# Mode weights arranged during the attention, and a depthwise buffer, its outputs and its stores laid out anew

## The chip, the cores and the metric

One core of a Trainium2 chip runs the whole program in one launch. The metric is the device time of that launch in microseconds. The engines are PE (TensorE, with its weight loads PEld), DVE (VectorE), ACT (ScalarE), POOL (GpSimd) and SP (SyncE, which here only issues transfers). All data is fp32.

## What is computed

An image `x` of 256 x 256 tokens with 128 channels passes four layers, each with a group normalization ahead of it and a residual behind it:

```python
x = x + _L0_conv_ref(_gn(x), ...)   # attention of each image row over a row of kv_x, 4 heads of 32
x = x + _L1_conv_ref(_gn(x), ...)   # 16 Fourier modes along rows and along columns, mixed by w1, w2; then an MLP
x = x + _L2_conv_ref(_gn(x), ...)   # one-channel convolutions and a pointwise chain
x = x + _L3_conv_ref(_gn(x), ...)   # two depthwise 7x7 convolutions, gate, softplus, then a product with W_out
```

Two parts matter here. In layer 1 each of 16 modes per axis multiplies by a complex 128 x 128 matrix, taken from `w1` and `w2`, whose shape is (128 in, 128 out, 16 modes, 2 parts). In layer 3 the result per token is

```python
h_final = jnp.exp(log_h[-1])        # a softplus of (conv_B(x) * sigmoid(conv_gate(x)))
return h_final @ W_out + b_out
```

## The kernel before

The stages follow one another, with a barrier of all engines between them: statistics (to about 99 us), `attention` (to 1955 us), `spectra` (to 2081 us), the mixing of modes, the MLP in two halves, the one-channel part, the pointwise part (to about 3850 us) and `depthwise_layer` (to the end).

**Attention.** One image row after the other, in a software pipeline written out by hand; PE's order, and the waits that other engines signal, set the pace. POOL does three things per row, in this order: `add_mask(n + 2, 0)`, `spread_sums(n - 1)`, `add_mask(n + 2, 1)`. SP loads `x`, `kv_x` and the mask four rows ahead and stores the row before last.

**Spectra.** SP streams the whole of `x1` (64 tiles of 512 KB, 12 in flight) while PE takes its modes along the other axis and transposes it for DVE's statistics. A quad is 4 tiles. At the start POOL loads `w1` and `w2` (2 MB each, L623) into `l_w`, and then rearranges them into `wcat` (L627 to L629): per axis and mode the blocks -imaginary, real, imaginary of 128 x 128, which `mix_modes_and_prepare_mlp` needs.

**Depthwise layer.** The convolution is a product over patches of 8 x 8 tokens (64 "spots"). Work goes in 8 blocks of 128 patches. Per block PE makes 32 groups of 4 channels (`conv(g)`, 16 matmul instructions each), and `copy_raw` puts them into `raw` (128 partitions, 128 lines of 128 numbers). In even blocks a line of `raw` is a channel, and `turn` takes a column of it for one patch, `raw[:, :, patch]`, numbers 512 bytes apart; in odd blocks a line is a patch, and `turn` takes a line. A unit `u` is 8 patches, 16 units per block, 128 in all. Per unit: `turn(u)` (8 transposes into `p_turn`), ACT's gate in three passes over 512 numbers, DVE's `gated`, `magnitude` and, two units later, `softplus` into `hid`; then `project` (the product with `W_out`, 8 PE instructions) and `residual` on DVE, which adds `xr`, to which POOL has added the bias. While unit `u` is turned, PE convolves two groups of the next block. The last block has no convolutions beside it: units 112 to 127 are a tail.

`softplus` writes `hid` spot by spot (one number each 128 bytes), and `project` takes 4 spots along x. So 4 stores of 32 partitions carry pieces of 512 bytes, as 4 loads do for the residual. In each turn of SP's loop `load_residual(u - 6)` comes ahead of `store(u - 10)`, and both wait for `added`, which `residual` signals. `residual(w)` waits for the store of `w - 4`, since `outs` has 4 buffers.

## Time and profile before

| | us |
|---|---|
| runs of the kernel before: median of 3 | 4745.81 |
| the three runs | 4656.36, 4745.81, 4747.08 |
| the profiled execution | 4665.72 |
| its span on the core | 4663.7 |
| busy: PE, PEld | 4324.7, 3310.7 |
| busy: DVE, ACT, POOL | 3407.1, 2858.4, 2102.6 |

A row of the timeline is: start, duration, engine, line, operation, output <- inputs, number of instructions, and in brackets the idle time ahead of it and what ended it. PE's durations include the way through the array, so they overlap; the distance between starts is the pace.

### The profile page before, as it was taken

Reading aid. Unit: us, or ns where it says so; the run is one execution under the profiler, and the core shown is the slowest. Engines: PE = TensorE matmul, PEld = TensorE weight load, DVE = VectorE, ACT = ScalarE, POOL = GpSimd, SP = SyncE. Lnnn points to the kernel's source line nnn. Section 1 sums busy time; section 2 is a strip of 40 time slices with the busy share of each in tenths; the row PEclk is TensorE's granted clock in tenths of the full one; section 3 lists DMA queues with packets and bytes.
Section 4 is the critical chain, followed back from the end, with each engine's and each line's share of the span. In section 5 each row is a group of like instructions: output and inputs, shape, how many; then the busy total and the mean of one; then the engine's idle time right before and its main releaser. Section 6 shows DMA issues by size and latency. Waiting matters only on the chain. (4 is left out here: it accounts for less than half of the span.)

```text
span 4663.7 us, 108212 instructions
## 1 busy us (share of the span) xinstructions
PE 4324.7 (93%) x35238; PEld 3310.7 (71%) x35238; DVE 3407.1 (73%) x10109; ACT 2858.4 (61%) x7950; POOL 2102.6 (45%) x1792
## 2 busy tenths in 40 slices
PE   5999999999999999877999989999739997999995
PEld 5777777777777777646677757777414447999995
DVE  7888888888888888663666656666339993667665
ACT  0888888888888888513333333333317882666664
POOL 0777777777777777513233313333016650222222
PEclk8999999999999999899999989999869998999997
DMA  7222222222222222385222222221847887999994
GB/s 317 69 77 77 80 77 79 78 76 80 77 76 80 77 77 80 130 292 183 68 73 71 72 83 71 73 71 64 301 164 254 295 279 254 278 286 294 288 294 113
DMA packets 726507, 679.49 MB, mean 146 GB/s; under 512 B 59029, under 2 KB 609172, under 8 KB 717399
## 3 DMA queue, kind: packets, MB, share of 16 engines
q1 hardware_dynamic: 710507, 643.38, 45.0%
q10 hardware_dynamic: 11645, 15.81, 1.0%
q0 software_dynamic: 3808, 13.47, 0.7%
q8 instruction: 288, 4.72, 0.4%
q14 instruction: 259, 2.12, 0.2%
HBM read 473.14 MB, written 199.29 MB: 144 GB/s over the span
## 5 line engine op out<-in xcount | busy, mean ns | idle before, releaser
L325 POOL TENSOR_TENSOR at_bias<-at_tri,at_mask 128x1024 f32<-128x1024 f32 x512 | 1204.6, 2375 | 115.7 <-DMA at_mask<-in_L_conv_mask_bias_dram 111.1
L465 ACT ACTIVATE at_probs<-at_neg_s,at_neg_max 128x256 f32<-128x256 f32 x2048 | 1012.9, 504 | 0.5 <-DVE at_neg_max L509 0.5
L509 DVE CUSTOM_DVE_ANT_0 at_neg_s<-at_p_s,at_bias 128x256 f32<-128x256 f32 x2048 | 761.9, 419 | 17.9 <-PE at_p_s L367 3.6
L1008 ACT ACTIVATE ml_h<-ml_p_turns,l_b 128x512 f32<-128x512 f32 x384 | 263.9, 687 | 608.1 <-PE ml_p_turns L967 608.1
L380 PE MATMUL at_p_t<-all_ident,at_probs 128*128 128x128 f32 x4096 | 614.1, 273 | 1.1 <-DVE at_probs_t L517 0.6
L976 PEld LDWEIGHTS ml_p<-l_w1s,ml_h 128*128 128x128 f32 x4096 | 471.9, 192 | 52.7 <-issue 52.7
L380 PEld LDWEIGHTS at_p_t<-all_ident,at_probs 128*128 128x128 f32 x4096 | 487.3, 141 | 28.3 <-ACT at_probs L465 2.6
L967 PE MATMUL ml_p_turns<-ml_h,l_w 128*128 128x512 f32 x1024 | 486.2, 598 | 2.3 <-DVE ml_h L1041 2.3
L976 PE MATMUL ml_p<-l_w1s,ml_h 128*128 128x128 f32 x4096 | 484.6, 277 | 0.8 <-issue 0.8
L1109 POOL TENSOR_TENSOR ml_x2t<-ml_z,ml_xb 128x512 f32<-128x512 f32 x128 | 163.3, 1276 | 678.3 <-DVE ml_z L1075 678.3
L2036 POOL TENSOR_TENSOR dw_room<-dw_room,all_b_plain 128x512 f32<-128x512 f32 x128 | 175.6, 1372 | 598.5 <-DMA dw_room<-x3t 598.5
L465 ACT ACTIVATION_READ_ACCUMULATOR at_probs<-at_neg_s,at_neg_max 128x1 f32 x2048 | 403.4, 197 | 0.0
L517 DVE COPY at_probs_t<-at_p_t 128x512 f32<-128x512 f32 x512 | 352.7, 689 | 4.6 <-PE at_p_t L380 0.6
L317 POOL COPY at_spread<-at_parts 128x256 f32<-128x256 f32 x256 | 102.2, 399 | 533.8 <-DVE at_parts L523 533.8
L2069 DVE SCALAR_TENSOR_TENSOR dw_hid<-dw_room 128x512 f32<-128x512 f32 x128 | 145.8, 1139 | 213.1 <-ACT dw_room L1965 213.1
L455 ACT ACTIVATE at_probs_t<-at_p_t 128x512 f32<-128x512 f32 x512 | 300.3, 586 | 0.8 <-PE at_p_t L380 0.8
L367 PE MATMUL at_p_s<-at_keys,at_queries 32*128 32x256 f32 x4096 | 294.2, 401 | 0.0
L393 PE MATMUL at_p_out<-at_probs_t,at_vs 128*32 128x256 f32 x4096 | 274.1, 385 | 1.1 <-DVE at_x1s L545 1.1
L1047 DVE TENSOR_SCALAR ml_h<-ml_p_turns,l_b 128x512 f32<-128x512 f32 x128 | 96.1, 750 | 244.3 <-PE ml_p L976 241.8
L967 PEld LDWEIGHTS ml_p_turns<-ml_h,l_w 128*128 128x128 f32 x1024 | 176.7, 192 | 132.9 <-issue 128.0
L1863 PE MATMUL dw_p_conv<-dw_xw,all_kept 128*128 128x128 f32 x2048 | 252.8, 275 | 10.2 <-DMA dw_xw<-planes 6.1
L1863 PE MATMUL dw_p_conv<-dw_xw,dw_wts 128*128 128x128 f32 x2048 | 251.3, 274 | 0.0
(232 smaller groups left out, 9225.7 us busy)
## 6 DMA issues: line engine op xcount, KB each, us to landing
dw_xw<-planes SPq DMA_DIRECT2D x128, 528.0 KB, 4.7
dw_wts<-patch_w SPq DMA_DIRECT2D x128, 512.0 KB, 6.0
planes<-pw_plane SPq DMA_DIRECT2D x128, 264.0 KB, 3.1
in_xs<-in_x_dram SPq DMA_DIRECT2D x32, 1024.0 KB, 7.7
at_xs<-in_x_dram SPq DMA_DIRECT2D x256, 128.0 KB, 2.3
at_kvs<-in_L_conv_kv_x_dram SPq DMA_DIRECT2D x256, 128.0 KB, 2.3
at_mask<-in_L_conv_mask_bias_dram SPq DMA_DIRECT2D x256, 128.0 KB, 3.2
x<-at_x1s SPq DMA_DIRECT2D x256, 128.0 KB, 1.8
```

The costliest lines, as they stand in the source:

```text
L325: pool.tensor_tensor(bias[:, n % 2, part], tri[:, part], mask[:, n % 4].unsqueeze(1).broadcast_to((128, 4, COLS)), ALU.add).then_inc(maske ...
L367: mm = pe.matmul(p_s[h][:, qh, :], queries[ch, n % 2, qh * 128:(qh + 1) * 128], keys[ch, n % 2, :], start=True, stop=True)
L380: mm = pe.transpose(p_t[h % 2][:, kh, qh * 128:(qh + 1) * 128], probs[:, h, qh, kh * 128:(kh + 1) * 128], ident[:, :])
L393: pe.matmul(p_out[ch, 0, :], vs[:, n % 4, kh, ch], probs_t[:, n % 3, h, kh, :], start=kh == 0, stop=kh == HALVES - 1)
L455: act.activation(probs_t[:, n % 3, h], p_t[1][:, :, :], ACT.Copy).then_inc(odd_read, 1)
L465: e = act.activation(probs[:, h, qh, :], neg_s[:, n % 2, h, qh, :], ACT.Exp, bias=neg_max[:, n % 2, i:i + 1], scale=-1.0, accum_out=sums[: ...
L509: t = dve.tensor_tensor_reduce(neg_s[:, n % 2, h, qh, :], p_s[h][:, qh, :], bias[:, n % 2, i, :], -1.0, 3.0e38, ALU.add, ALU.min, neg_max[ ...
L517: dve.tensor_copy(probs_t[:, n % 3, h], p_t[0][:, :, :]).then_inc(even_read, 1)
L967: mm = pe.matmul(bank_of(hidden_use(t, b))[:, :], w0[:, b * 128:(b + 1) * 128], h[:, t % 2, :], start=True, stop=True)
L976: mm = pe.matmul(p_2[:, j, :], h1[:, b, j * 128:(j + 1) * 128], w1c[:, b, :], start=b == 0, stop=b == blocks - 1)
L1008: act.activation(h1[:, b, :], bank_of(hidden_use(t, b))[:, :], ACT.Relu, bias=b0[:, b:b + 1]).then_inc(relu_act, 1)
L1863: mm = pe.matmul(p_conv[g % 2][:, j, :], weights, xw[:, k % 3, :, g % 2 * 4 + j, side:side + PX], start=side == 0, stop=side == 1)
```

## The change

1. `attention` gets the work on the mode weights. SP loads `w1` into `mode_w` in turn n = 2 and `w2` in turn n = 104 of its loop. POOL makes one of the 96 blocks of `wcat` in every second row from n = 8 (axis 0) and from n = 112 (axis 1), between `spread_sums` and the second `add_mask`. `spectra` loses its POOL part.
2. `raw` has lines of 132 numbers (528 bytes), of which 128 are used.
3. The spots are numbered x first, then y. `p_turn` is written by each transpose in runs of 4 numbers (4 spots along y), the runs 64 bytes apart; before, a transpose wrote 128 numbers in a row. `hid` has y innermost; `softplus` is two instructions of 256 numbers, which write runs of 16 numbers.
4. `project` takes 4 spots along y, so a partition of `outs` holds 4 neighbouring tokens: one store of 128 partitions, in pieces of 2 KB. The residual still comes in 4 loads of 512-byte pieces, now each over 128 partitions.
5. The statistics of layer 2 lie in a tensor allocated earlier (no instruction differs).

```diff
+                if n == 2:
+                    sp.dma_start(mode_w[:, :, :, :], mode_weights[0]).then_inc(w_loaded, 16)
+                if n == 8 + 2 * 3 * MODES:
+                    sp.wait_ge(w_copied, 3 * MODES)
+                    sp.dma_start(mode_w[:, :, :, :], mode_weights[1]).then_inc(w_loaded, 16)
...
+            def copy_weights(axis, i):
+                mode, part = i // 3, i % 3
+                pool.wait_ge(w_loaded, 16 * (axis + 1))
+                dst, src = wcat[:, axis, mode, part, :], mode_w[:, :, mode, (1, 0, 1)[part]]
+                if part == 0:
+                    pool.tensor_scalar(dst, src, -1.0, None, ALU.mult).then_inc(w_copied, 1)
+                else:
+                    pool.tensor_copy(dst, src).then_inc(w_copied, 1)
...
+                for axis in range(2):
+                    i = n - 8 - axis * (2 * 3 * MODES + 8)
+                    if 0 <= i < 2 * 3 * MODES and i % 2 == 0:
+                        copy_weights(axis, i // 2)
...
-            for axis in range(2):
-                pool.dma_start(w[:, axis], weights[axis]).then_inc(w_loaded, 16)
-            pool.wait_ge(w_loaded, 32)
-            for axis in range(2):
-                by_mode = w[:, axis].rearrange("p o k z -> p z k o")
-                pool.tensor_scalar(wcat[:, axis, :, 0, :], by_mode[:, 1], -1.0, None, ALU.mult)
-                pool.tensor_copy(wcat[:, axis, :, 1, :], by_mode[:, 0])
-                pool.tensor_copy(wcat[:, axis, :, 2, :], by_mode[:, 1])
...
-        raw = m.sb("raw", [128, CH, BLOCK_PY * PX])
+        raw = m.sb("raw", [128, CH, BLOCK_PY * PX + 4])
-        hid = m.sb("hid", [128, 2, SPOTS, PX])
+        hid = m.sb("hid", [128, 2, SPOTS // 4, PX, 4])
-        p_turn = [m.ps(f"p_turn{i}", [128, PATCH, 2 * SPOTS]) for i in range(2)]
+        p_turn = [m.ps(f"p_turn{i}", [128, 2, 2, SPOTS // 4, 4, 4]) for i in range(2)]
...
-                for d in range(4):
-                    sp.dma_start(out[0, r * PATCH + y:r * PATCH + y + 4].rearrange("y (a d) c -> d a y c", d=PATCH)[x + d],
-                                 outs[d * PX:(d + 1) * PX, w % 4]).then_inc(stored[w % 4], 16)
+                cells = out[0, r * PATCH + y:r * PATCH + y + 4].rearrange("y (a d) c -> a y d c", d=PATCH)
+                sp.dma_start(cells[:, :, x:x + 4].rearrange("a y d c -> a y (d c)"),
+                             outs[:, w % 4].rearrange("p d c -> p (d c)")).then_inc(stored[w % 4], 16)
...
-                    cells = raw[:, patch, :] if u // units % 2 else raw[:, :, patch]
-                    mm = pe.transpose(p_turn[u % 2][:, i, :], cells, ident[:, :])
+                    cells = raw[:, patch, 0:CH] if u // units % 2 else raw[:, :, patch]
+                    places = p_turn[u % 2][:, i // 4, :, :, i % 4].rearrange("p f s y -> p (f s) y")
+                    mm = pe.transpose(places, cells, ident[:, :])
...
-                dve.scalar_tensor_tensor(out=hid[:, r % 2, :, x:x + PATCH].rearrange("p s a -> p a s"), in0=bt[:, u % 3],
-                                         scalar=0.0, in1=soft[:, u % 2], op0=ALU.max, op1=ALU.add).then_inc(hid_made, 1)
+                for half in range(2):
+                    part, at = slice(half * BANK // 2, (half + 1) * BANK // 2), x + half * 4
+                    done = dve.scalar_tensor_tensor(out=hid[:, r % 2, :, at:at + 4].rearrange("p s a y -> p s (a y)"),
+                                                    in0=bt[:, u % 3, part].rearrange("p (s n) -> p s n", n=16), scalar=0.0,
+                                                    in1=soft[:, u % 2, part].rearrange("p (s n) -> p s n", n=16),
+                                                    op0=ALU.max, op1=ALU.add)
+                done.then_inc(hid_made, 1)
```

How the change moves instructions, on the two engines that it touches most. A row is a line, an operation, output <- inputs and its size.

POOL at the first blocks of `wcat` in the attention, of the kernel after (`at_bias` is `add_mask`, `at_spread` is `spread_sums`, `l_wcat` is `wcat`):

```order
L341 TENSOR_TENSOR at_bias<-at_tri,at_mask 128x1024 x2
L324 COPY at_spread<-at_parts 128x256
L332 TENSOR_SCALAR l_wcat<-at_mode_w 128x128
L341 TENSOR_TENSOR at_bias<-at_tri,at_mask 128x1024 x2
L324 COPY at_spread<-at_parts 128x256
L341 TENSOR_TENSOR at_bias<-at_tri,at_mask 128x1024 x2
L324 COPY at_spread<-at_parts 128x256
L334 COPY l_wcat<-at_mode_w 128x128
```

Before, the rows of `at_bias` and `at_spread` alternate without those of `l_wcat`, which stand in `spectra` as six instructions of 128x2048.

SP's last transfers, of the kernel before (`dw_room<-x3t` is `load_residual`, `out_dram<-dw_room` is `store`):

```order
L1819 DMA out_dram<-dw_room 32x4x128 x4
L1813 DMA dw_room<-x3t 32x4x128 x4
L1819 DMA out_dram<-dw_room 32x4x128 x20
L1823 DMA out_dram<-dw_og_final 3x3x128
L1825 DMA out_dram<-dw_og_final 3x4x128
```

and of the kernel after:

```order
L1832 DMA out_dram<-dw_room 32x4x512
L1826 DMA dw_room<-x3t 128x1x128 x4
L1832 DMA out_dram<-dw_room 32x4x512 x5
L1836 DMA out_dram<-dw_og_final 3x3x128
L1838 DMA out_dram<-dw_og_final 3x4x128
```

The order is the same, but a store is one transfer where it was four; the last run of stores is 5 transfers where it was 20.

## Rows read from the trace of the kernel before

**Rows 1.** The page: its first line, the span on the core.
```profile
span 4663.7 us, 108212 instructions
```

**Rows 2.** Windows: stretch, busy PE, PEld, DVE, ACT, POOL, granted clock, DMA share, GB/s.
```profile
1000.00:1500.00 500.00, 500.00 (x5053) 388.92 (x5053) 437.13 (x1702) 435.23 (x1545) 355.79 (x211) 1.00 0.28 78
...
3945.10:4557.80 612.70, 612.66 (x5329) 612.36 (x5330) 411.91 (x549) 395.34 (x668) 148.14 (x107) 1.00 1.01 283
4557.80:4634.30 76.50, 44.20 (x257) 40.55 (x256) 53.81 (x68) 48.23 (x83) 22.44 (x17) 0.78 0.44 113
```

**Rows 3.** Timeline of POOL in the attention.
```profile
1915.62 0.40 POOL L317 COPY at_spread<-at_parts 128x256 f32<-128x256 f32 x1 [1.96 <-DVE at_parts L523]
...
1922.64 0.40 POOL L317 COPY at_spread<-at_parts 128x256 f32<-128x256 f32 x1 [1.96 <-DVE at_parts L523]
```

**Rows 4.** Timeline in `spectra`: PE's first tiles and two quads; POOL's weights.
```profile
1960.10 1.94 PE L643 MATMUL sp_p_turn<-all_ident,sp_xs 128*128 128x128 f32 x8 [8.59 <-DMA sp_xs<-x]
1971.26 4.83 PE L643 MATMUL sp_p_turn<-all_ident,sp_xs 128*128 128x128 f32 x24 [9.22 <-DMA sp_xs<-x]
...
1987.06 2.26 PE L643 MATMUL sp_p_turn<-all_ident,sp_xs 128*128 128x128 f32 x16 [0.61 <-DVE l_stats L686]
...
1993.68 2.26 PE L643 MATMUL sp_p_turn<-all_ident,sp_xs 128*128 128x128 f32 x16 [0.60 <-DVE l_stats L686]
...
1971.26 7.09 POOL L627 TENSOR_SCALAR l_wcat<-l_w 128x2048 f32<-128x2048 f32 x1 [13.85 <-DMA l_w<-in_L_conv_w_dram]
```

**Rows 5.** Timeline of PE, depthwise layer, two turns in an even block.
```profile
4342.42 1.33 PE L1876 MATMUL dw_p_turn<-all_ident,dw_raw 128*128 128x128 f32 x8
...
4348.06 1.33 PE L1876 MATMUL dw_p_turn<-all_ident,dw_raw 128*128 128x128 f32 x8
```

**Rows 6.** The same in an odd block.
```profile
4403.30 1.04 PE L1876 MATMUL dw_p_turn<-all_ident,dw_raw 128*128 128x128 f32 x8
...
4408.64 1.04 PE L1876 MATMUL dw_p_turn<-all_ident,dw_raw 128*128 128x128 f32 x8
```

**Rows 7.** Lines: instructions by form; busy us, mean ns; idle before, releaser.
```profile
L1863 PE MATMUL dw_p_conv<-dw_xw,all_kept 128*128 128x128 f32 x2048 | 252.8, 275 | 10.2 <-DMA dw_xw<-planes 6.1 <-DVE dw_raw L1926 4.1
L1926 DVE COPY dw_raw<-dw_p_conv 128x512 f32<-128x512 f32 x64 | 43.5, 680 | 37.2 <-PE dw_p_conv L1863 37.2
L1924 DVE COPY dw_raw<-dw_p_conv 128x512 f32<-128x512 f32 x64 | 43.2, 675 | 7.2 <-PE dw_p_conv L1863 7.2
...
L1257 DVE COPY all_kept<-tp_p_w 128x256 f32<-128x256 f32 x32 | 18.8, 589 | 58.0 <-PE tp_p_w L1226 58.0
...
L551 DVE COPY at_kvt<-at_p_in 128x256 f32<-128x256 f32 x256 | 106.2, 415 | 0.0
```

**Rows 8.** One line or tile: count, duration ns min/median/max, first and last start.
```profile
L1876 PEld LDWEIGHTS dw_p_turn<-all_ident,dw_raw x1024: 137/225/268, 3945.1 to 4627.7; 128*128 128x128 f32 x171
...
L2061 DVE SCALAR_TENSOR_TENSOR dw_room<-dw_room x128: 691/694/1761, 3949.8 to 4632.1; 128x512 f32<-128x512 f32 x128
...
L2069 DVE SCALAR_TENSOR_TENSOR dw_hid<-dw_room x128: 1012/1068/2066, 3958.5 to 4635.7; 128x512 f32<-128x512 f32 x128
```

**Rows 9.** The chain that ended last, in the tail: start, us, what.
```profile
4583.69 2.04 PE dw_p_out L1886 x8
...
4589.52 0.85 issue
...
4593.28 1.95 PE dw_p_out L1886 x8
```

**Rows 10.** Timeline of SP and DVE at the very end.
```profile
4647.86 0.69 DVE L2077 TENSOR_TENSOR dw_room<-dw_p_out,dw_room 128x512 f32<-128x512 f32 x1 [3.11 <-DMA out_dram<-dw_room]
4648.33 9.71 SPq L1819 DMA_DIRECT2D out_dram<-dw_room  x20
...
4651.70 0.69 DVE L2077 TENSOR_TENSOR dw_room<-dw_p_out,dw_room 128x512 f32<-128x512 f32 x1 [3.15 <-DMA out_dram<-dw_room]
4659.48 0.79 SPq L1823 DMA_DIRECT2D out_dram<-dw_og_final  x1
```

More of the change, by code:

```diff
@@ L201, in _, with attention @@
             act.activation(std[:, :], var[:, :], ACT.Sqrt, bias=epsc[:, :]).then_inc(act_step, 1)
-def attention(nc, x, kv, tri_bias, mask_bias, wq, wk, wv, wg, wo, ident, scale, shift, x1, forward, spec_rows, rows=ROWS):
+def attention(nc, x, kv, tri_bias, mask_bias, wq, wk, wv, wg, wo, ident, scale, shift, x1, forward, spec_rows, mode_weights, wcat, rows=ROWS):
     xv, kvv = x[0].rearrange("r (h p) c -> r p h c", p=128), kv[0].rearrange("r (h p) c -> r p h c", p=128)
@@ L588, with spectra @@
 LN_EPS = 1e-5
-def spectra(nc, x1, forward, ident, stats, spec, weights, w, wcat):
+def spectra(nc, x1, forward, ident, stats, spec):
     quads, group, rows = ROWS // 16, 4, 4
@@ L1129, in fourier_layer @@
         b0 = m.sb("b0", [128, HIDDEN // 128])
[L1130 to L1131 removed]
+        stats_out = m.sb("stats2", [128, TOKENS // BANK, 6])
+        with nc.sbuf_tensor("l1_wcat", [128, 2, MODES, 3, CH], fp) as wcat:
+            attend(wcat)
             with nc.sbuf_tensor("l1_stats", [128, TOKENS // BANK, 6], fp) as stats:
[L1133 removed]
+                spectra(nc, x1, consts["forward"], ident, stats, spec[1])
                 group_norm_coefficients(nc, "l1", stats[:, :, :].rearrange("p a b -> p (a b)"), group_mean,
@@ L1892, in turn_origin @@
                 for i in range(2):
-                    mm = pe.transpose(p_turn[0][:, i, :], og_xs[:, i, :], ident[:, :])
+                    mm = pe.transpose(og_turn[:, i, :], og_xs[:, i, :], ident[:, :])
                 mm.then_inc(og_turned, 1)
@@ L1925, in copy_raw @@
             else:
-                done = copy(raw[:, c:c + 4, :], p_conv[g % 2][:, :, :])
+                done = copy(raw[:, c:c + 4, 0:BLOCK_PY * PX], p_conv[g % 2][:, :, :])
             done.then_inc(copied, 1)
@@ L1946, in gate_first @@
                     act.wait_ge(bt_made, u - 1)
-                act.activation(gate[:, u % 2], p_turn[u % 2][:, :, SPOTS:2 * SPOTS], ACT.Exp,
+                act.activation(gate[:, u % 2].rearrange("p (h n) -> p h n", h=2), by_patch[u % 2][:, :, 1], ACT.Exp,
                                bias=f_shift[:, 1:2], scale=nscale[:, :]).then_inc(gate_step, 1)
@@ L2053, in gated @@
                     dve.wait_ge(hid_made, u - 2)
-                dve.scalar_tensor_tensor(out=bt[:, u % 3], in0=p_turn[u % 2][:, :, 0:SPOTS], scalar=f_shift[:, 0:1],
-                                         in1=gate[:, u % 2], op0=ALU.add, op1=ALU.mult).then_inc(bt_made, 1)
+                dve.scalar_tensor_tensor(out=bt[:, u % 3].rearrange("p (h n) -> p h n", h=2), in0=by_patch[u % 2][:, :, 0],
+                                         scalar=f_shift[:, 0:1], in1=gate[:, u % 2].rearrange("p (h n) -> p h n", h=2),
+                                         op0=ALU.add, op1=ALU.mult).then_inc(bt_made, 1)
             def magnitude(u):
@@ L2090, in origin_window @@
                     chained(dve.tensor_copy(og_win[:, :, first:first + k],
-                                            p_turn[0][:, part, base:base + span * k].rearrange("p (y d) -> p y d", d=k)))
+                                            og_turn[:, part, base:base + span * k].rearrange("p (y d) -> p y d", d=k)))
                 chained(dve.tensor_reduce(og_sum, og_kern[:, 1, :], mybir.AxisListType.X, ALU.add))
```

49 lines of the change are left out of this document (24 added, 25 removed).

## The prediction

> **What bounds the kernel now.** The profiled execution took 4665.7 us, of which the span on the core is 4663.7 [rows 1]; all sums below are made against the 4665.7. It belongs with the lowest of the three runs (4656.36); the other two lie near 4746, and nothing in one profile says why. The same saving taken off the median of 4745.81 gives a time about 80 us higher, which the range has to hold.
>
> I read the windows first, stage by stage, since the change touches three stages with different limits. The attention keeps PE busy for all of 500 us in 500 us, with the DMA engines at 0.28 [rows 2]: PE alone sets it. The depthwise layer with convolutions (612.7 us) also has PE busy throughout, but there the DMA share is 1.01: two limits lie side by side, and PE's is the one that binds, since its convolutions waited for windows in all 6.1 us [rows 7]. The tail behind it (4557.8 to 4634.3) is bound by neither, PE is busy 44.20 of 76.50 us at a granted clock of 0.78 of the full one [rows 2]; there a chain through four engines counts. Then I read timelines of the places that the change names.
>
> **The change part by part.**
>
> *Weights in the attention.* POOL's period is that of an image row: from one `spread_sums` to the next 1922.64 - 1915.62 = 7.02 us, with 1.96 us of idle time ahead of it [rows 3]. The change puts one block of 128 numbers per partition behind `spread_sums` in every second row. The costlier kind took 7.09 us for 2048 numbers [rows 4], so 0.44 us for 128; with a fixed part the nearest row is the copy of 256 numbers, 0.40 us [rows 3]. I take 0.3 to 0.6 us per block, 96 times, on an engine that has 1.96 us to spare each time. What is queued behind it is the second `add_mask`, whose result DVE wants one row later. Cost on the path: 0. Without the cover it would be 96 x 0.5 = 48 us.
>
> The loads of 2 MB are issued by SP. The first stands behind the load of row 6, when only prefetches are under way. The second stands in the steady state. Both together, with tiles of `x1` between them, were awaited 13.85 us in `spectra` [rows 4]; I take half, 7 us, as the most that one can delay the transfers behind it. Those fetch four rows ahead of SP's own turn, some two periods or 14 us before they are used, at a DMA share of 0.28. Cost: 0, at most 7 us once.
>
> *Weights out of spectra.* This is the clearest gain. PE turned the first tile at 1960.10, then waited 9.22 us, until 1971.26, for the second [rows 4]. POOL's first instruction on the weights starts at the same 1971.26: the 4 MB had stood between the first and the second tile of `x1`. From then on PE and DVE pace a quad at 1993.68 - 1987.06 = 6.62 us, 1.66 us per tile of 512 KB [rows 4], with no wait for a transfer. Without the 4 MB the second tile comes about one tile's time behind the first. Saved: 9.2 less some 0.7 us of waiting = 8.5 us. Bounds: 4 us if tiles then come too slowly for a while, 9.2 us.
>
> *Lines of 528 bytes.* The distance from one turn to the next is 4348.06 - 4342.42 = 5.64 us in an even block [rows 5] and 4408.64 - 4403.30 = 5.34 us in an odd one [rows 6]. The eight transposes take 1.33 and 1.04 us from first start to last end; the difference is the whole difference of the periods. What differs is how the weight load reads `raw`: 137 ns at best, 225 ns for the median [rows 8], since most units turn single numbers 512 bytes apart. Units 0 to 111 have convolutions beside them, 64 of them in even blocks. If the reads 528 bytes apart run as contiguous ones do, 64 x 0.30 = 19.2 us is saved; if the cost comes from each number lying alone, nothing is. No row shows a stride of 528. That the cost belongs to a multiple of a large power of two is my reading of the number 36 ns per 128 columns: that is 0.3 ns per number, less than DVE loses on scattered numbers (0.7 ns, below). I take 19.2, with more doubt than for any other term.
>
> The Trainium skill (SBUF — State Buffer, Specifications) says that SBUF has lines of 16 bytes, that at least two hits per line are needed for full bandwidth, and that each cross to a new line is paid. By it a step of 528 bytes is as bad as one of 512, and the sum would lack the 19.2 us. That the strided units are slow agrees with it; no row here separates it from the other reading.
>
> *Runs of 16 bytes in `p_turn`.* All 1024 transposes now write 4 numbers, then skip. No row has PE writing in this way. Lower bound 0: DVE writes runs of 16 bytes, 512 bytes apart, in 675 ns where contiguous lines take 680 (L1924 and L1926, [rows 7]). Upper bound: DVE writes 256 single scattered numbers in 589 ns and 256 contiguous ones in 415 (L1257 and L551, [rows 7]), 0.68 ns per number, 87 ns per transpose, 89 us in all. The runs are of four, so the first row is nearer; I take 0.
>
> *Softplus in two halves.* Alone it takes 1.07 us (median) against 0.69 us for `magnitude`, which has the same size and writes contiguously [rows 8]: the scattered write costs 0.38 us. Two halves in runs of 64 bytes should take 0.7 to 0.85 us. With convolutions beside it, DVE is busy 411.91 of 612.70 us [rows 2]: hidden. In the tail `softplus` stands on the chain. Two units take one turn of it, 4593.28 - 4583.69 = 9.59 us, and its piece is the 0.85 us "issue" between ACT and the gated product [rows 9]. ACT's last gate pass ends not much earlier, so I count 0.2 us for each of 8 turns: 1.6 us. ACT and DVE read `p_turn` in longer pieces than before: 0.
>
> *Stores.* A transfer costs SP 9.71 / 20 = 0.486 us to issue [rows 10]. A unit takes 8 of them, 3.9 us, afterwards 5, 2.4 us. While units last 5.3 us this hides. At the end it doesn't: the last `residual` instructions stand 4651.70 - 4647.86 = 3.84 us apart and wait for stores [rows 10], which is just 8 issues. Three such steps shorten by 1.46 us each: 4.4 us. Behind the last one SP still had to issue 20 stores before it could wait and go on to the origin's, at 4659.48, 7.8 us later [rows 10]. Afterwards: 0.69 for `residual`, 0.49 for one issue, about 1.4 us to land (4659.48 less the end of the issues, 4648.33 + 9.71): 2.6 us, 5.2 saved. Together 9.6 us; bounds 6 and 13.
>
> *Sum.* 8.5 + 19.2 + 1.6 + 9.6 = 38.9 us; 4665.7 - 38.9 = 4626.8, say 4627 us, 0.8% less.
>
> **The rivals.**
>
> *The stride does not help.* 38.9 - 19.2 = 19.7 us saved: 4646 us. For it: the loss is there for any scattered access that the rows show. Against: its size per number differs. Chance 0.22.
>
> *PE's scattered writes cost.* This one ends on the other side. The place is `turn`, on the path of the whole stage. At the upper bound of 87 ns per transpose the time is 4627 + 89 = 4716 us, 1.1% slower; it decides from 38.9 us / 1024 = 38 ns per transpose on. Against it speaks L1924. Chance 0.12, a quarter of that for a price above the bound.
>
> The Trainium skill (PSUM — Partial Sum Buffer, Specifications) gives PSUM lines of 8 bytes and says that "any non-contiguous AP slows matmuls significantly". It names no price; by its word this rival would be the likeliest. No row of this case has a matmul whose output skips, so the trace neither supports nor refutes it.
>
> *The gains elsewhere don't come.* If `spectra` is then bound by its transfers and the tail by the clock, since PE idles between units there (granted 0.78 [rows 2]), I keep 19.2 + 4 + 6 = 29 us: 4637 us. Chance 0.08. *The attention pays*: a late mask or row holds PE up; at half a microsecond per block 4627 + 48 = 4675 us, no change. Against it: 1.96 us of idle time, three times what is put in. Chance 0.04.
>
> *More than the sum.* The depthwise layer runs at a DMA share of 1.01. If the two runs near 4746 are executions in which transfers fell behind there, stores in a quarter as many pieces relieve just that, and the time stays at 4627 where it was 4746. The profile can't show it. Chance 0.10.
>
> **How the numbers follow.** The forecast as summed has chance 0.44: 4627 us, its own range from its bounds 4612 to 4640. The cases above add 4637, 4646, 4675 and 4716. The range reaches below to 4600 and above to 4720: this holds the rival on the other side at its bound, and also the forecast taken off the median of the runs, 4745.8 - 38.9 = 4707. About 2% is what a measurement of this kernel can tell from no change. Faster by over 2% needs the last case, or a saving of 93 us against the profile, which no part can give: 0.11. Slower by over 2% needs the scattered writes well above their bound, or two losses at once: 0.04. Within 2%: 0.85.
>
> **What would show it.** In `spectra` the second tile is turned within some 3 us of the first, and the stage is 8 to 9 us shorter. Turns in even blocks stand 5.34 us apart, as in odd ones, and the weight loads of `turn` have a median near 140 ns; if they stay at 225 the stride was not it. If odd blocks take more than 5.34 us, PE's writes pay. `softplus` shows 256 instructions near 0.42 us. The last residuals stand some 2.4 us apart. POOL's idle time ahead of `spread_sums` falls from 1.96 to about 1.5 us in every second row, and an image row still takes 7.02 us; if it doesn't, the attention pays. The prediction is wrong if PE's period per unit moves to any value but 5.34, or if PE starts to wait for transfers in the depthwise layer once it asks for them 5% faster.

## The result, and the profile after

The changed kernel took 4711.23 us (median of four runs, 4710.27 to 4711.56). Four runs of the kernel before, beside them, gave 4656.36, 4657.54, 4745.81 and 4747.08. Against the two low ones the changed kernel is slower by a ratio of 1.0116, with a 95% interval of 1.0092 to 1.0141; its four runs lie between the two levels of before. The forecast was 4627 us, faster. It was wrong by 84 us, and nearly all of that sits in one stage that the prediction never looked at. Executions of either kernel fall on two levels of time, some 80 us apart, by the clock that TensorE has in that stage; I call them the high clock and the low clock.

The profiled execution of the changed kernel took 4711.11 us:

```profile
span 4709.3 us, 108044 instructions
```

I laid the first and last start of each stage's main instruction beside those of before. Up to the end of the MLP the changed kernel is ahead by 14.3 us, 10.2 of them in `spectra`. Then comes the stage of the row taps and patch weights (`row_taps_and_patch_weights`, whose products change only in the order of the spots): it ends 66.9 us behind, so it lost 81.2. Behind it the depthwise convolutions gain 11.1 and the tail 10.0 us. With 0.2 gained in the stages between, -14.3 + 81.2 - 0.2 - 11.1 - 10.0 = +45.6, which is the difference of the spans.

The windows of this stage, first of before, then of after (stretch, busy time of PE, PEld, DVE, ACT and POOL, granted clock, DMA share, GB/s): the wait for `w`, the entry, the body.

```profile
3290.00:3302.00 12.00, 0.00 (x0) 0.00 (x0) 0.00 (x0) 0.00 (x0) 2.76 (x5) 0.50 1.00 312
3302.00:3306.00 4.00, 3.57 (x24) 0.88 (x24) 0.40 (x2) 0.69 (x1) 0.00 (x0) 0.50 0.80 292
3308.00:3395.00 87.00, 87.00 (x481) 47.43 (x474) 31.01 (x60) 42.69 (x86) 0.00 (x0) 1.00 0.92 357
```

```profile
3276.00:3288.00 12.00, 0.00 (x0) 0.00 (x0) 0.00 (x0) 0.00 (x0) 2.92 (x6) 0.50 0.99 316
3288.00:3292.00 4.00, 3.37 (x24) 0.88 (x24) 0.40 (x2) 0.69 (x1) 0.00 (x0) 0.50 0.74 279
3294.00:3455.00 161.00, 161.00 (x464) 78.17 (x456) 29.58 (x59) 49.64 (x86) 0.00 (x0) 0.50 0.58 193
```

PE waits, then works through the same entry at 1.2 GHz (0.50) in both. In before the clock then goes to 2.4 GHz (1.00) and is there for the whole window of 87 us; in after it stays at 1.2 GHz for the whole body, though PE is never idle in it. Two tiles of each, in the timeline of PE (start, us), show what that costs: 2.92 us per tile and 5.58.

```profile
3342.40 1.06 PE L1216 MATMUL tp_p_out<-tp_xs,tp_ws 128*32 128x512 f32 x8
3343.40 1.99 PE L1226 MATMUL tp_p_w<-tp_kt,tp_sel 49*128 49x256 f32 x8
3345.32 1.07 PE L1216 MATMUL tp_p_out<-tp_xs,tp_ws 128*32 128x512 f32 x8
```

```profile
3343.88 1.93 PE L1227 MATMUL tp_p_out<-tp_xs,tp_ws 128*32 128x512 f32 x8
3345.75 3.78 PE L1237 MATMUL tp_p_w<-tp_kt,tp_sel 49*128 49x256 f32 x8
3349.46 1.94 PE L1227 MATMUL tp_p_out<-tp_xs,tp_ws 128*32 128x512 f32 x8
```

**The other places**, as named in the prediction. In `spectra` three tiles are turned without a wait, where [rows 4] had 9.22 us behind the first; a quad then takes the same 6.63 us:

```profile
1960.56 4.48 PE L652 MATMUL sp_p_turn<-all_ident,sp_xs 128*128 128x128 f32 x24 [8.39 <-DMA sp_xs<-x]
...
1970.74 2.26 PE L652 MATMUL sp_p_turn<-all_ident,sp_xs 128*128 128x128 f32 x16 [0.61 <-DVE l_stats L695]
...
1977.37 2.26 PE L652 MATMUL sp_p_turn<-all_ident,sp_xs 128*128 128x128 f32 x16 [0.61 <-DVE l_stats L695]
```

POOL in the attention, beside [rows 3]: the block of weights takes 0.40 us in every second row, the idle time ahead of the next `spread_sums` falls from 1.96 to 1.60, and the row still takes 7.02 us.

```profile
1039.69 0.40 POOL L324 COPY at_spread<-at_parts 128x256 f32<-128x256 f32 x1 [1.96 <-DVE at_parts L543]
1040.03 0.40 POOL L334 COPY l_wcat<-at_mode_w 128x128 f32<-128x128 f32 x1
...
1046.71 0.40 POOL L324 COPY at_spread<-at_parts 128x256 f32<-128x256 f32 x1 [1.60 <-DVE at_parts L543]
```

Turns in an odd block (first two rows) and in an even one: 5.34 us apart as in [rows 6], and 5.43 us where [rows 5] had 5.64. The third fence has the weight loads of the turns in that even block, then those of an odd block of the kernel before, which read contiguous numbers (count, ns min/median/max, first and last start): medians of 210 and 141 ns. The same even block of the kernel before has 256 ns. The 225 of [rows 8] is the median over even and odd blocks together and is the duration of neither. The last row is `softplus`.

```profile
4283.27 1.04 PE L1890 MATMUL dw_p_turn<-all_ident,dw_raw 128*128 128x128 f32 x8
4288.61 1.04 PE L1890 MATMUL dw_p_turn<-all_ident,dw_raw 128*128 128x128 f32 x8
```

```profile
4369.66 1.12 PE L1890 MATMUL dw_p_turn<-all_ident,dw_raw 128*128 128x128 f32 x8
4375.09 1.12 PE L1890 MATMUL dw_p_turn<-all_ident,dw_raw 128*128 128x128 f32 x8
```

```profile
L1890 PEld LDWEIGHTS dw_p_turn<-all_ident,dw_raw x123: 195/210/216, 4353.9 to 4435.5; 128*128 128x128 f32 x123
L1876 PEld LDWEIGHTS dw_p_turn<-all_ident,dw_raw x112: 139/141/142, 4387.2 to 4457.4; 128*128 128x128 f32 x112
L2085 DVE SCALAR_TENSOR_TENSOR dw_hid<-dw_room x256: 407/424/1530, 4024.5 to 4688.6; 128x256 f32<-128x256 f32 x128
```

The last rows of the tail, DVE, POOL and SP's queue, beside [rows 10]: `residual` comes every 3.13 to 3.34 us (3.84 before, 2.4 forecast) and waits for POOL, POOL for the load of the residuals, and SP needs 2.55 us to issue four of those.

```profile
4695.47 0.69 DVE L2096 TENSOR_TENSOR dw_room<-dw_p_out,dw_room 128x512 f32<-128x512 f32 x1 [2.65 <-POOL dw_room L2049]
4695.58 0.60 SPq L1832 DMA_DIRECT2D out_dram<-dw_room  x1
4696.23 2.55 SPq L1826 DMA_DIRECT2D dw_room<-x3t  x4
...
4698.60 0.69 DVE L2096 TENSOR_TENSOR dw_room<-dw_p_out,dw_room 128x512 f32<-128x512 f32 x1 [2.44 <-POOL dw_room L2049]
...
4700.59 1.26 POOL L2049 TENSOR_TENSOR dw_room<-dw_room,all_b_plain 128x512 f32<-128x512 f32 x1 [2.08 <-DMA dw_room<-x3t]
4701.94 0.69 DVE L2096 TENSOR_TENSOR dw_room<-dw_p_out,dw_room 128x512 f32<-128x512 f32 x1 [2.65 <-POOL dw_room L2049]
4705.11 0.81 SPq L1836 DMA_DIRECT2D out_dram<-dw_og_final  x1
```

### The profile page after: what moved, and what is told of

It reads as the page before. It is cut to its first block and busy times, and to the rows that moved or that the text cites. A ratio compares the mean times of both kernels' runs of the same rounds, so it can differ in the third digit from the quotient of the medians.

```text
span 4709.3 us, 108044 instructions
## 1 busy us (share of the span) xinstructions
PE 4392.3 (93%) x35238; PEld 3333.5 (71%) x35238; DVE 3396.1 (72%) x10237; ACT 2864.2 (61%) x7950; POOL 2106.8 (45%) x1880
## 5 line engine op out<-in xcount | busy, mean ns | idle before, releaser
L2085 DVE SCALAR_TENSOR_TENSOR dw_hid<-dw_room 128x256 f32<-128x256 f32 x256 | 142.5, 597 | 209.6 <-ACT dw_room L1978 209.4
```

## The experiments

The theory (T): both kernels have the same two levels, which are the taps stage at the high or the low clock; it is drawn at the stage's entry, after PE has waited; and at equal clock the change saves what was forecast. Rivals: something in the change, the new order of the spots or the moment at which the stage starts, keeps the clock low in every run (P) or in more of them than before (O); the levels are of the transfers (D).

### Both kernels again, and both with PE at work while it waited

`e1_before` and `e2_after` are the two kernels unchanged. The other two add this to `row_taps_and_patch_weights` of each:

```diff
+            for i in range(56):
+                pe.matmul(p_w[i % 4][:, 0, 0, :], ident[:, :], ident[:, :], start=True, stop=True)
             pe.wait_ge(w_loaded, 16)
```

> The kernel before once more, unchanged. What is disputed is where its two levels, 4656 and 4747 us, lie. Theory T: they are one stage, that of the row taps and patch weights, at one of TensorE's two clocks: 1.2 GHz throughout (granted clock 0.50) or 2.4 GHz from its start on (1.00). The changed kernel's stage ran at 0.50 throughout and took 80 us longer than the same stage of the profiled execution of before. Then single runs of this kernel fall at about 4656 or about 4747 with nothing between, and their mean granted clocks over the span fall in two groups, near 0.964 and near 0.948. Rival D: the two levels come from transfers (DMA), and the clock has nothing to do with them; then the mean clocks of the runs at both levels agree within 0.003.

> The changed kernel once more, unchanged. Theory T with a clock that is decided at the stage's entry in each run: if it is a matter of chance, some of these runs reach the high level and then take about 4711 - 80 = 4631 us. Rival P: something in the changed kernel (the new numbering of the spots, or the moment at which the stage starts) keeps the clock at 0.50 in every run; then all runs lie within 2 us of 4711 and no mean clock is above 0.950.

> The changed kernel, with 56 matmuls of 128x128 on the identity matrix (their result is overwritten and never read) on TensorE at the start of the stage of the row taps, where it otherwise waits 15 us for the weights' transfer. At 0.50 one takes about 0.43 us, 24 us in all at most, less if the clock rises. Theory T (the stage is slow because TensorE came into it at 1.2 GHz after a wait, and its own work does not bring the clock up): every run falls to 4620 to 4640 us, and the stage's granted clock is 1.00 from its first tile on. Rival P (the new order of the spots makes the stage's products slower or holds the clock down while they run): the run stays at 4705 to 4720 us, with 0.50 in the stage whatever happened ahead of it.

> The kernel before with the same 56 matmuls at the same place. Theory T: no run near 4747 is left; all lie between 4655 and 4670 us, and the changed kernel with them is 0.6 to 0.9 per cent faster than this one (30 to 40 us: 14 of spectra and the stages behind it, 11 of the depthwise layer, 10 of the tail, by the two traces). Rival D (the two levels are of the transfers): both levels are still there.

Measured. Of 44 runs of the kernel before, five lay at 4737 to 4745 with mean clocks of 0.945 to 0.947, three between 4690 and 4705 (0.954 to 0.958), the others at 4653 to 4678 (0.961 to 0.966). Of 12 of the changed kernel, four lay at 4708 to 4713 (0.948, 0.949) and eight at 4625 to 4642 (0.965 to 0.967). So the changed kernel does reach the high clock, and there it is faster: 0.9931 of before, interval 0.9907 to 0.9955. D falls, as the mean clock goes with the level, and so does P. "Nothing between" was wrong. The profile of `e2_after` fell at the low clock too, with 0.50 over the same 161 us.

With the 56 matmuls the changed kernel took 4626 to 4632 us in nine of ten runs, one took 4658.5 (0.960); before took 4655 to 4674 in eleven of twelve, one 4710 (0.955). The lowest level is gone in both. The timeline of PE in `e3_after_warm` has the 56 where the wait was (a matmul in fp32 is shown as two), and the stage then runs at 2.4 GHz from its first tile, as the windows behind it show.

```profile
3274.11 14.35 PE L1243 MATMUL tp_p_w<-all_ident 128*128 128x128 f32 x112 [2.50 <-PEq L78]
3288.56 0.24 PE L1246 MATMUL tp_p_small<-all_coef,tp_w 128*32 128x1 f32 x8
3289.13 1.92 PE L1227 MATMUL tp_p_out<-tp_xs,tp_ws 128*32 128x512 f32 x16 [0.33 <-DVE tp_ws L1300]
```

```profile
3274.00:3288.50 14.50, 14.35 (x112) 14.18 (x112) 0.00 (x0) 0.00 (x0) 3.95 (x7) 0.88 0.95 295
3289.00:3292.00 3.00, 2.30 (x22) 0.69 (x22) 0.59 (x4) 0.69 (x1) 0.00 (x0) 1.00 0.73 231
3294.00:3375.00 81.00, 81.00 (x446) 42.46 (x444) 29.00 (x56) 40.25 (x80) 0.00 (x0) 1.00 0.96 379
```

These two profiles give the change at equal clock, from the first and last starts of each stage's main line:

| us | before, `e4` | after, `e3` | difference | forecast |
|---|---|---|---|---|
| attention | 1818.0 | 1817.9 | -0.1 | 0 |
| spectra, first to last turn | 115.5 | 105.0 | -10.5 | -8.5 |
| taps stage | 93.5 | 93.1 | -0.4 | 0 |
| depthwise, first to last convolution | 680.7 | 666.0 | -14.7 | -19.2 |
| from there to the end | 104.4 | 94.2 | -10.2 | -11.2 |
| span | 4661.5 | 4624.4 | -37.1 | -38.9 |

The rows without the span add up to -35.9; the other 1.2 us lie in the stages between. The equal taps stages also say that the new order of the spots costs the products nothing. By the medians of the runs the two differ by 34.6 us, 0.7%, inside the 0.6 to 0.9% that were expected.

### Does the change raise the odds of the low clock?

> The changed kernel, unchanged. So far 8 of its 16 runs were near 4710 us (mean clock 0.948) and 8 between 4625 and 4642 (0.965 to 0.967), while of the kernel before 7 of some 69 were near 4743 (0.947). Chance theory: the two levels are drawn anew in every run, for both kernels with the same odds, and the share here comes near that of before on this chip. Rival O (the change itself raises the odds of the low clock): a third or more of these runs near 4710, with at most a tenth of the kernel before near 4743.

`h2_before_order` and `h3_after_old_order` exchange one line between the kernels (shown for `h2`):

```diff
-                    oy, ox = divmod(spot + i, PATCH)
+                    ox, oy = divmod(spot + i, PATCH)
```

> The kernel before with only the new numbering of the spots in the stage of the row taps (the patch weights come out in another order than its depthwise layer reads them, so the output differs). If the new order of the selector's slices raises the odds of the low clock, a third or more of the runs are near 4743; if not, at most one or two of twelve are. The runs at the high clock lie at 4655 to 4672 us either way.

> The changed kernel with the old numbering of the spots (output differs for the same reason). If the new order raises the odds, nearly no run is near 4710; if something else in the change does it, a third or more still are. The runs at the high clock lie at 4625 to 4642 us.

`h4_after_weights_late` is the changed kernel with the edit of `f8_loads_in_spectra`, below, and without the matmuls.

> The changed kernel with the mode weights loaded a second time during spectra, unread, so that the stage of the row taps starts 11 us later, about where it does in the kernel before. If the moment of the start decides (it is the only thing that stands otherwise than in the changed kernel at this stage), nearly no run falls to the low clock (4722 us) and all lie at 4636 to 4650; if not, the share is that of the changed kernel.

Measured on one chip, runs at the low clock: before 3 of 22 (4739 to 4748), the changed kernel 1 of 6 (4709), `h2` 2 of 12 (4743, 4748), `h3` 2 of 12 (4708, 4715), `h4` 1 of 6 (4721). Neither the order nor the moment moves the share by more than so few runs can tell. One further run each of `h1` and `h3` lay between (4656, 4677). Two runs are left out of these counts: one of before took 8469 us at a mean clock of 0.490, one of `h1` 15286 us at 0.316; neither was profiled, and what happened in them is not known. The profile of `h1_after` fell into the low level by itself, and shows the same stage at the low clock, where a product took 617 ns in before:

```profile
L1227 PE MATMUL tp_p_out<-tp_xs,tp_ws x256: 1030/1061/1062, 3289.6 to 3457.0; 128*32 128x512 f32 x128
```

Over all comparisons beside the first, the kernels without the matmuls were at the low level in 19 of 136 runs, those with them in none of 54 (six of these lay 20 to 55 us above their level, with clocks of 0.955 to 0.962). Split by kernel, those 19 are 11 of 100 runs of before (with `h2`) and 8 of 36 of the changed kernel (with `h3` and `h4`); with the first comparison it is 13 of 104 and 12 of 40. So the level is drawn anew in each run of both kernels, but that the odds are the same is not shown: rival O, in the form that the change raises them, is open. The first comparison, four of four, fits equal odds badly, though before had two of four beside it. Open are also the runs between the levels: none of them was profiled.

The profiles give one hint. In the three at the low clock (the first, `e2`, `h1`) PE's first product in the stage starts 32.6 to 32.7 us after the MLP's last one, in the five that reached the high clock without the matmuls (the first of before, `e1`, `h2`, `h3`, `h4`) 32.0 to 32.4 us. A few tenths of a microsecond at the entry may decide, then, and a change elsewhere can move them. But all three are the unaltered changed kernel, of which no profile fell at the high clock, so this does not tell the cause from the kernel.

### The lines of 528 bytes

From here on every kernel has the 56 matmuls, so that the clock disturbs no comparison, and is read by its profile.

```diff
f1_line512
-        raw = m.sb("raw", [128, CH, BLOCK_PY * PX + 4])
+        raw = m.sb("raw", [128, CH, BLOCK_PY * PX])
```

```diff
f5_line516
-        raw = m.sb("raw", [128, CH, BLOCK_PY * PX + 4])
+        raw = m.sb("raw", [128, CH, BLOCK_PY * PX + 1])
```

```diff
f2_before_line528
-        raw = m.sb("raw", [128, CH, BLOCK_PY * PX])
+        raw = m.sb("raw", [128, CH, BLOCK_PY * PX + 4])
...
-                    cells = raw[:, patch, :] if u // units % 2 else raw[:, :, patch]
+                    cells = raw[:, patch, 0:CH] if u // units % 2 else raw[:, :, patch]
...
-                done = copy(raw[:, c:c + 4, :], p_conv[g % 2][:, :, :])
+                done = copy(raw[:, c:c + 4, 0:BLOCK_PY * PX], p_conv[g % 2][:, :, :])
```

> The changed kernel with the 56 matmuls, and with the depthwise buffer's lines 512 bytes apart again (the 16-byte spread in PSUM stays). Read from its profile, beside 4624 us of the same kernel with lines of 528 bytes. Theory S (the step between the lines is the whole of what the even blocks gained): the even blocks' period goes from 5.43 back to 5.64 us, so the 64 even units cost 64 x 0.21 = 13 us more and the depthwise layer's convolutions take 679 us instead of 666. Rival W (the even blocks' turns lost something to the 16-byte runs in PSUM, which is why 5.34 wasn't reached): the period comes out above 5.64, near 5.73, and the layer at 685 us.

> The kernel before with the 56 matmuls, and of the change only the lines of 528 bytes; PSUM is written in order. Beside 4661 us of the same kernel with lines of 512 bytes. Theory S: the period of the even blocks goes from 5.64 to 5.43 us, 13 us in all, as in the changed kernel. Rival W: without the 16-byte runs in PSUM the even blocks reach the odd ones' 5.34 us, as the prediction had it, and 19 us are saved.

> The changed kernel with the 56 matmuls and lines 516 bytes apart (129 numbers in place of 132). Theory S1 (any step that is not 512 bytes helps as much as 528): period of the even blocks 5.43 us. Rival S2 (the number of different 16-byte places that successive reads fall on counts, a step of 516 moves the start by 4 bytes only and stays four times in one of them): the period lies between 5.43 and 5.64, near 5.6. Rival S3 (a step that isn't a multiple of 16 bytes costs reads): above 5.64.

Two turns of an even block and the weight loads of the turns in that block, for lines of 512 bytes (`f1`), then 516 (`f5`), then 528 with PSUM written in order (`f2`):

```profile
4333.99 1.34 PE L1892 MATMUL dw_p_turn<-all_ident,dw_raw 128*128 128x128 f32 x8
4339.63 1.33 PE L1892 MATMUL dw_p_turn<-all_ident,dw_raw 128*128 128x128 f32 x8
...
L1892 PEld LDWEIGHTS dw_p_turn<-all_ident,dw_raw x123: 220/256/268, 4283.8 to 4368.7; 128*128 128x128 f32 x123
```

```profile
4326.40 1.19 PE L1892 MATMUL dw_p_turn<-all_ident,dw_raw 128*128 128x128 f32 x8
4331.89 1.18 PE L1892 MATMUL dw_p_turn<-all_ident,dw_raw 128*128 128x128 f32 x8
...
L1892 PEld LDWEIGHTS dw_p_turn<-all_ident,dw_raw x121: 200/218/238, 4277.9 to 4360.0; 128*128 128x128 f32 x121
```

```profile
4325.24 1.12 PE L1878 MATMUL dw_p_turn<-all_ident,dw_raw 128*128 128x128 f32 x8
4330.67 1.12 PE L1878 MATMUL dw_p_turn<-all_ident,dw_raw 128*128 128x128 f32 x8
...
L1878 PEld LDWEIGHTS dw_p_turn<-all_ident,dw_raw x122: 195/210/214, 4287.8 to 4370.1; 128*128 128x128 f32 x122
```

The period is 5.64, 5.49 (5.46 to 5.54 over the block) and 5.43 us. Theory S holds and W falls: the step alone makes 5.64 into 5.43, with or without the 16-byte runs in PSUM, which cost PE nothing in either kind of block. In `f1` the convolutions of the layer took 679.5 us, as S had it (679). A step of 516 gets most of it, 0.15 of 0.21 us; S1 is wrong, and S2 has the interval but not the size (near 5.6). Not every step but 512 is equal, and none of those tried reads as contiguous numbers do. In `f2` the layer's convolutions took 671.5 us, 9.2 less than in `e4_before_warm` and not 13: a dozen periods were 0.2 to 0.7 us longer than their neighbours, where `e4` had two such. Why is not shown.

### What spectra gained

```diff
+        again = m.sb("again", [128, 2, CH, MODES, 2])
...
+        @block.gpsimd
+        def _(pool):
+            for axis in range(2):
+                pool.dma_start(again[:, axis], weights[axis]).then_inc(again_loaded, 16)
+            pool.wait_ge(again_loaded, 32)
```

> The changed kernel with the 56 matmuls, and the mode weights loaded a second time during spectra, by the same queue as in the kernel before, into room that nobody reads (nothing is arranged there, and the output is that of the changed kernel). It tells apart what the 10 us gained in spectra were. Theory A (GpSimd's arranging, whose large instructions lay beside VectorE's): spectra stays at 105 us from its first to its last turn, and the total within 2 us of 4624. Rival B (the transfers of the weights, 4 MB beside spectra's own): spectra goes back to 115 us and the total to 4634.

Measured: from the first to the last turn 115.3 us, as in before, and 4637.2 us. The wait behind the first tile is back:

```profile
1960.51 1.94 PE L660 MATMUL sp_p_turn<-all_ident,sp_xs 128*128 128x128 f32 x8 [8.51 <-DMA sp_xs<-x]
...
1971.38 5.38 PE L660 MATMUL sp_p_turn<-all_ident,sp_xs 128*128 128x128 f32 x24 [8.93 <-DMA sp_xs<-x]
```

The transfers were all of it, GpSimd's large instructions nothing: over all profiles the stage takes 115.0 to 115.5 us with the 4 MB in it and 104.8 to 105.8 without.

### The tail, and softplus beside GpSimd

`g0_after_warm` is `e3_after_warm` again. `f3_late_room` loads the last six residuals early (`rest_of(w)` is `xr[:, w % 4]`, and for the last six windows 512 numbers of `xw`), and `f7_copy_first` also changes VectorE's order; `f9_no_bias` removes GpSimd's addition.

```diff
f3_late_room
+                if w == total - 6:
+                    sp.wait_ge(conved, streamed)
-                    sp.dma_start(xr[:, w % 4, d], cells[(1 - x) * SHIFT + d][:, y:y + 4]).then_inc(r_loaded[w % 4], 16)
+                    sp.dma_start(rest_of(w)[:, d], cells[(1 - x) * SHIFT + d][:, y:y + 4]).then_inc(landed, 16)
...
+                if 0 <= u - (total - 14) < 6:
+                    load_residual(u + 8)
```

```diff
f7_copy_first
-                if 2 <= u < total + 2:
-                    softplus(u - 2)
                 if lead + 2 * u < streamed:
                     copy_raw(dve, lead + 2 * u, dve.tensor_copy, even_copied)
+                if 2 <= u < total + 2:
+                    softplus(u - 2)
```

```diff
f9_no_bias
-                pool.tensor_tensor(xr[:, w % 4], xr[:, w % 4], b_plain.unsqueeze(1).broadcast_to((128, 4, CH)),
-                                   ALU.add).then_inc(biased, 1)
...
-                dve.wait_ge(biased, w + 1)
+                dve.wait_ge(r_loaded[w % 4], 64 * (w // 4 + 1))
```

> The changed kernel with the 56 matmuls again, as the kernel to compare the next two with on the same chip: 4624 to 4633 us, 0.993 of before.

> The changed kernel with the 56 matmuls, and the residuals of the last six windows loaded early, into the convolutions' input buffer, which is free by then; so SyncE has their 24 transfers behind it before the last units, and only stores to issue at the end. Theory L (the last residuals stand 3.3 us apart, and not the 2.4 us of the prediction, because SyncE issues four loads and a store for each in 3.1 us or more and GpSimd's bias waits for them): the last six follow each other at 1.2 to 1.5 us, and 6 to 9 us are saved: 4617 to 4621 us where the kernel without this takes 4626. Rival G (GpSimd's 1.27 us and what it does to VectorE set the pace): less than 3 us are saved.

> As f3_late_room, and VectorE copies the convolution's result ahead of softplus in each unit, where softplus came first. Theory C (where a block ends, PE sometimes waits 0.5 to 0.6 us for a copy that stands behind a softplus slowed by GpSimd): the four or so periods of 5.98 to 6.07 us among 128 go, some 2 us in all, and nothing else moves. Rival H (the later softplus holds up the hidden rows at the end, or the gate): the time stays or grows by some us.

> The changed kernel with the 56 matmuls, without GpSimd's 128 instructions that add the output bias to the residuals (so the output lacks the bias). It tells what they cost beside VectorE. Theory C: softplus's halves never exceed 0.45 us (their mean of 0.60 us falls to 0.41), no period at a block's end is over 5.5 us, and the end is 1 to 4 us shorter because a residual waits for its load alone; 4618 to 4624 us in all. Rival: the halves keep their mean of 0.6 us, and it is something else that slows them.

Measured. `g0`: 4632.8 us, 0.9948 of before (0.9920 to 0.9976), two of its eleven runs at 4677 and 4684. `f3`: 4625.1 us, 0.9916 (0.9899 to 0.9933). From the last convolution to the end it took 89.9 us against 94.2 in both `e3` and `g0`, 4.3 less. One profile each does not fix that number: the changed kernel's tail, with nothing altered in it, took 91.6 (`f8`) to 97.0 us (the first profile). By the medians of the runs `f3` saves 7.7 us against `g0` beside it and 5.0 against `e3`. The last residuals follow each other at 0.9 to 1.7 us and wait for PE:

```profile
4609.03 0.69 DVE L2118 TENSOR_TENSOR dw_room<-dw_p_out,dw_xw 128x512 f32<-128x512 f32 x1 [0.49 <-PE dw_p_out L1921]
4610.76 0.69 DVE L2118 TENSOR_TENSOR dw_room<-dw_p_out,dw_xw 128x512 f32<-128x512 f32 x1 [1.04 <-PE dw_p_out L1921]
4611.65 0.69 DVE L2118 TENSOR_TENSOR dw_room<-dw_p_out,dw_xw 128x512 f32<-128x512 f32 x1 [0.20 <-PE dw_p_out L1921]
```

In `f9_no_bias`, where GpSimd adds nothing but SP issues the same loads, the last residuals still stand 3.2 us apart. So L named the right cause, and G's instruction does not set this pace; what the early loads save is some 2 to 8 us by these numbers, since once the loads are there, PE's last projections bind. `f7`: 4626.5 us, 0.9936 (0.9914 to 0.9957), the same as `f3`; each period at a block's end is 5.38 to 5.48 us, where `e3` had two of 5.78 to 5.98 and one of 6.07. That agrees with C, but one profile does not show that the order did it: `f3`, which keeps the old order, had only one such period (5.70). Gain or none, it is worth less than a run differs from the next. `f9`: a span of 4620.4 us (4622.2 for the run, of 4618 to 4624 expected), softplus at one duration, and the last residual:

```profile
L2085 DVE SCALAR_TENSOR_TENSOR dw_hid<-dw_room x256: 414/422/427, 3945.7 to 4598.4; 128x256 f32<-128x256 f32 x128
...
4612.98 0.69 DVE L2096 TENSOR_TENSOR dw_room<-dw_p_out,dw_room 128x512 f32<-128x512 f32 x1 [2.52 <-DMA out_dram<-dw_room]
```

The mean of `softplus` is 0.42 us, against 0.60 in the changed kernel and 0.63 in `g0`: GpSimd's addition is what slows it. No period at a block's end is over 5.48. With GpSimd's addition in place a pair looks like this, in the timeline of the changed kernel: 1.81 us where it takes 0.76 alone, and the copy that PE's turn waits for starts only behind it.

```profile
4177.05 1.27 POOL L2049 TENSOR_TENSOR dw_room<-dw_room,all_b_plain 128x512 f32<-128x512 f32 x1 [4.26 <-DMA dw_room<-x3t]
4177.13 1.81 DVE L2085 SCALAR_TENSOR_TENSOR dw_hid<-dw_room 128x256 f32<-128x256 f32 x2 [1.13 <-ACT dw_room L1978]
...
4178.86 0.68 DVE L1939 COPY dw_raw<-dw_p_conv 128x512 f32<-128x512 f32 x1
...
4179.64 1.20 PE L1890 MATMUL dw_p_turn<-all_ident,dw_raw 128*128 128x128 f32 x8 [0.45 <-DVE dw_raw L1939]
```

The Trainium skill (SBUF — State Buffer, SBUF: two separate sides) says that a VectorE instruction with two inputs in SBUF and a GpSimd instruction that reads SBUF exclude each other for a whole instruction. The delay here, 1.81 - 0.76 = 1.05 us beside an instruction of 1.27 us that began 0.08 us earlier, agrees.

## Why the prediction was wrong, point by point

**The step that failed** is the first: "all sums below are made against the 4665.7", with "nothing in one profile says why" the other two runs lie near 4746. That took the clock of the taps stage from one execution and carried it over to the changed kernel without a reason. What the runs showed in its place: the changed kernel's four runs had this stage at 1.2 GHz, 81.2 us longer. The sum was near for an execution at the high clock (38.9 forecast, 37.1 measured); which level the changed kernel would be in was not part of it. The trace held the clue: a stage that is entered at 0.50 after a wait, with the clock rising only 4 us into it. At the low clock its 161 us stand where 87 would. I took the windows of the stages that the diff touches, and this one, where the diff changes one line, was never opened. The one guess at the levels, transfers that fall behind in the depthwise layer, was wrong; the line that took the saving off the other level, 4745.8 - 38.9 = 4707, came within 4 us of the 4711 that was measured, but it was given as a bound of the range and no chance of its own.

**That before's upper level is this stage** is inferred, since no profile of before fell there: its mean clock, 0.945 to 0.947, is that of the changed kernel's profiled low level, its distance is 80 to 90 us, and it never came with the 56 matmuls. The sum agrees: a mean of 0.964 over 4664 us is 336 us at 0.50; with the 171.6 us that the stage's patch weights take at the low clock that makes 508 of 4744 us, a mean of 0.946.

**Weights in the attention:** right. 0.40 us per block in an idle time that falls by 0.36 us; the stage is unchanged. **Weights out of spectra:** mechanism right, shown by `f8`; 10.5 us rather than 8.5, above the bound of 9.2, since not only the second tile but those behind it came without a wait.

**Lines of 528 bytes:** mis-sized. The step was taken to make the reads as fast as contiguous ones, 64 x 0.30 = 19.2 us. It gave 0.21 us per unit, 13.4 us by that count and 14.7 us in the two profiles; over all profiles of the two kernels with this layer unaltered the convolutions take 678.8 to 680.7 us before and 666.0 to 668.2 after. The rule in the Trainium skill (SBUF — State Buffer, Specifications), by which each crossing to a new line is paid, had 528 no better than 512. Measured, both readings are half right: in an even block a weight load has a median of 256 ns at 512, 218 at 516 and 210 at 528, and 141 in an odd block, where the numbers are contiguous. A part of the loss belongs to the step, the larger part stays. The argument that led to the 19.2 had read the loss from the period, 36 ns per transpose. The load itself loses 115 ns, 0.9 ns per number, and most of that does not show in the period; so it was not less than what VectorE loses on scattered numbers (0.7), as the prediction had it. "Most units turn single numbers" was a misreading too: half of them do, and a median of 225 ns over both halves belongs to neither.

**Runs of 16 bytes in `p_turn`:** right, 0: 5.34 us in odd blocks, and `f1` and `f2` show the same for even ones. The Trainium skill (PSUM — Partial Sum Buffer, Specifications) says that any non-contiguous pattern slows matmuls much; for transposes that write four numbers and skip twelve, these runs do not agree.

**Softplus and stores:** the total from the last convolution to the end was near, 10.2 us against 11.2, and its parts were not. The last residuals were to be 2.4 us apart, from five transfers at 0.486 us. They are 3.3 apart, as a load now fills all 128 partitions and takes 2.55 / 4 = 0.64 us to issue, a store 0.60: the count was right and the price was taken from smaller transfers. That step gave 3 x 0.5 = 1.5 us and not 4.4. The end behind the last residual went from 7.8 to 3.2 us, 4.6 where 5.2 was forecast. The other 4.1 us came in the units before, where 1.6 was forecast: from the last convolution to the last turn 68.5 us in `e4` and 64.6 in `e3`. What shortened them is not shown, and this stretch differs by some 5 us between executions of one kernel (66.1 to 71.2 before, 62.2 to 67.4 after), so that the near total is in part luck.

## What to carry to other kernels

If the runs of an unchanged kernel lie on two levels, find the stage first: read the granted clock over the whole span, and above all where TensorE comes out of a wait into thin work, whether or not the change touches that stage. A sum of savings is made for each level, and compared at the same level; here 0.7% could be measured only so. A median over instructions of two kinds can be the duration of neither: take them apart first. A price for issuing a transfer, or for a stride, holds for the shape that it was read from.

## What the runs showed that was not expected

TensorE can be busy throughout a stage for 161 us and stay at 1.2 GHz. The same body, products of 32 columns and of 49 rows, kept 2.4 GHz to within 6 us of its last start in all fifteen profiles of executions that had reached this level at its start. Without the matmuls the clock rose there 2.7 to 3.9 us after the first product (five profiles), during or just behind the 16 instructions of products that follow one another there without a gap (3.2 to 3.6 us); in no profile did it rise later in the stage. The Trainium skill (TensorE: Matmul & The Clock Gate, Part 1: The HAM clock gate) explains a rise that comes at another moment in each run by a monitor whose phase is not tied to the kernel's; the two outcomes of one and the same entry agree with that. That a busy stage can miss the rise altogether is what these traces add.

56 idle products, 14.4 us in a wait that is there anyway, removed the lowest level in 54 runs. With them and the six early loads (`f3_late_room`) the kernel took 4625.1 us, 0.9916 of before. That beats the kernel before beyond its interval; against the changed kernel at the high clock (0.9931) the intervals overlap, and what it has over it for certain is the lowest level, gone.
